# A four-stage network on sixteen images: the front of the next image woven into the scan steps of this one

## The reference

```python
x = x + _L0_conv_ref(_gn(x), qkv_w, proj_w, proj_b)   # attention over 1024 pixels, 6 heads of 32
x = x + _L1_conv_ref(_gn(x), ...)   # selective scan, 4 directions, 192 channels x 16 states
x = x + _L2_conv_ref(_gn(x), ...)   # depthwise 3x3, the top 30 pixels of a channel keep their value
x = x + _L3_conv_ref(_gn(x), ...)   # gated chunked state-space layer, 12 heads
```

## Time and profile before

| | us |
|---|---|
| median of 3 runs | 14195.23 (14193.28 to 14201.19) |
| the profiled execution, its own time | 14205.94 |
| its span | 14204.1 |
| busy in it: PE / DVE / ACT / POOL | 8617.6 / 9455.2 / 4329.4 / 6226.0 |
| mean granted PE clock, share of 2.4 GHz | 0.708 |

### The profile page before, as it was taken

How to read it: one execution, slowest core, us unless ns; L and a number is a source line. 1 busy time by engine, 2 the same in 40 slices (tenths; PEclk the granted TensorE clock), 3 DMA queues, 4 the chain that set the end, 5 groups by cost and what they waited for, 6 DMA issues and landing times. The chain is left out here.

```text
span 14204.1 us, 88128 instructions
## 1 busy us (share of the span) xinstructions
PE 8617.6 (61%) x26672; PEld 2789.1 (20%) x26816; DVE 9455.2 (67%) x8214; ACT 4329.4 (30%) x4371; POOL 6226.0 (44%) x2937
## 2 busy tenths in 40 slices
PE   6475664746647466484664846648466484664846
PEld 2031221212212122121221312213122131221312
DVE  4856748567485674856758577585775857758576
ACT  2323233232332323323233232322323223232232
POOL 1815518155171551715417154271642716427164
PEclk8676776767767677676776767767676676776767
DMA  2505225052250512505135051340513405134061
GB/s 74 138 16 134 55 70 134 16 138 50 75 129 16 142 46 78 126 16 144 44 83 121 16 148 40 85 119 16 151 37 85 119 16 151 37 89 115 16 155 35
DMA packets 364229, 1164.38 MB, mean 82 GB/s; under 512 B 61487, under 2 KB 63039, under 8 KB 363599
## 3 DMA queue, kind: packets, MB, share of 16 engines
q1 hardware_dynamic: 358363, 1155.62, 32.3%
q10 hardware_dynamic: 3988, 1.01, 0.0%
q0 software_dynamic: 1248, 0.64, 0.0%
HBM read 959.86 MB, written 121.63 MB: 76 GB/s over the span
## 5 line engine op out<-in xcount | busy, mean ns | idle before, releaser
L799 PE MATMUL ps<-arena,sel_y 128*32 128x512 f32 x6144 | 2216.9, 888 | 3817.3 <-POOL arena L1048 3817.3
L1048 POOL TENSOR_TENSOR arena<-arena 128x1024 f32<-128x1024 f32 x1536 | 3721.7, 2449 | 29.4 <-DVE arena L995 29.4
L995 DVE TENSOR_TENSOR_SCAN arena<-ps,arena 128x1024 f32<-128x1024 f32 x1536 | 3475.8, 2284 | 66.9 <-POOL arena L1036 22.6
L913 ACT ACTIVATE ps<-arena,v_na 128x1024 f32<-128x1024 f32 x1536 | 1712.4, 1117 | 3797.8 <-DVE arena L995 3110.6
L1036 POOL TENSOR_TENSOR arena<-arena 128x1024 f32<-128x1024 f32 x512 | 1235.4, 2413 | 822.6 <-DMA arena<-scan_dtu 717.5
L799 PEld LDWEIGHTS ps<-arena,sel_y 128*32 128x32 f32 x6144 | 474.5, 151 | 5570.4 <-POOL arena L1048 3509.2
L617 DVE TENSOR_REDUCE arena<-ps 128x1 bf16<-128x1024 f32 x768 | 933.8, 1223 | 922.9 <-PE ps L480 922.4
L1028 POOL TENSOR_TENSOR arena<-arena,XN 128x1024 f32<-128x1024 f32 x32 | 75.2, 2350 | 2839.5 <-DVE arena L942 2839.5
L991 DVE TENSOR_TENSOR arena<-arena,ps 128x1024 f32<-128x1024 f32 x768 | 919.3, 1197 | 565.5 <-DMA arena<-scan_dtu 355.5
L597 ACT ACTIVATE arena<-ps 128x1024 f32<-128x1024 f32 x768 | 744.5, 1021 | 970.6 <-PE ps L532 970.6
L548 PE MATMUL ps<-arena 128*64 128x512 f32 x3072 | 773.0, 627 | 3.5 <-DVE arena L611 3.5
(11 more groups left out here) (213 smaller groups left out, 11961.2 us busy)
## 6 DMA issues: line engine op xcount, KB each, us to landing
arena<-scan_dt SPq DMA_DIRECT2D x768, 512.0 KB, 4.7
arena<-scan_dtu SPq DMA_DIRECT2D x768, 512.0 KB, 6.0
arena<-scan_bc SPq DMA_DIRECT2D x256, 512.0 KB, 6.2
arena<-arena SPq DMA_DIRECT2D x1152, 64.0 KB, 2.0
scan_dt<-arena SPq DMA_DIRECT2D x64, 512.0 KB, 10.9
scan_dtu<-arena SPq DMA_DIRECT2D x64, 512.0 KB, 8.9
scan_dt<-arena SPq DMA_DIRECT2D x64, 256.0 KB, 12.4
scan_dtu<-arena SPq DMA_DIRECT2D x64, 256.0 KB, 12.5
```

The lines of the kernel that those rows point to most:

```text
L799: mm = nc.tensor.matmul(ps[3][32 * q:32 * q + 32, HALF * h:HALF * h + HALF], sel_y[:, r, :], step[i % NBUF][:, HALF * h:HALF * h + HALF], ...
L913: nc.scalar.activation(ps[1 + i % 2][:], dtr[:, i // 2 % RING, :], ACT.Exp, scale=v_na[:, at:at + 1]).then_inc(m_da, 1)
L995: nc.vector.tensor_tensor_scan(step[i % NBUF][:, o], ps[1 + i % 2][:, o], step[i % NBUF][:, o], 0.0, ALU.mult, ALU.add).then_inc(m_h, 1)
L1048: pool.tensor_tensor(step[i % NBUF], step[i % NBUF], Cb[:, 2 * (k // 2) + f, :], ALU.mult).then_inc(m_hc, 1)
```

## The change

The front of an image (group norm, attention, group norm, scan setup) becomes, on each engine, a generator of 192 half steps: `front_sp`, `front_pe`, `front_act`, `front_dve`, `front_pool`. The scan of image b calls `next(front)` twice in each of its 96 steps on every engine, and what comes there is the front of image b + 1. Ahead of the loop the front of image 0 runs alone; the last pass computes a front for a seventeenth image (a copy of the first), which nothing uses.

- **Hand-over.** The image after attention (`after_attention`), the normalised one (`scan_source`), dt, dt * u, B and C go to DRAM in the front and are read back in the next pass; B, C, dt, dt * u had gone there before.
- **Attention.** q and k stay fp32 (QQ, KK), two heads a stack, on rows 0 to 31 and 64 to 95, with a row 32 (96) that holds the maximum and ones; so 12 projections of 512 columns with 24 matmuls instead of six with 12. No bf16 parts, none of the 72 small DMAs, no row copies. The scores of a head are one fp32 matmul of 33 rows (L637) instead of two bf16 ones. Rough scores read the upper half words of the same fp32 (QR, KR). A unit is 512 columns of two heads: PSUM is cut into four banks of 512 for the front, one of them for all rough scores (96 half-row maxima, L820, instead of 48 of 1024), one for sums of heads.
- **Steps.** One PSUM buffer for the decay instead of two (`decay(i + 1)` waits for scan i). b is always read from SBUF. DVE makes 42 inputs (L1073), POOL 54 (L1137). Eight step buffers, dt in a ring of two. PSUM bank `ps[3]` sums states as before.
- **Setup.** In the front: linear part by ACT, clamp and maximum by DVE with both operands in SBUF, all six dt * u by POOL.
- `conv_pool` waits for `f_out`, which SP raises when the front's stores have landed.

The table of half steps: attention's rough scores of the three pairs begin at 16, 52 and 88, units at 52 and 88 (one each two half steps) and 124 (one each half step), projections at 10, output projection at 142, setup from 149 to 184.

```diff
         def scan_pe(pe, front):
...
+            for i in range(NSTEP):
+                next(front)
+                if i % BATCH == 1 and i > BATCH:
+                    sums(i // BATCH - 1)
+                next(front)
+            sums(NSTEP // BATCH - 1)
...
         def scan_act(act, front):
+            def decay(i):
+                _, k, j, _, _, f = STEPS[i]
+                act.wait_ge(m_dtl[i // 2 % DTR], 16 * (i // 2 // DTR + 1))
+                if i:
+                    act.wait_ge(m_h, i)
+                at = 24 * k + 2 * j + f
+                nc.scalar.activation(ps[2][:], dtr[:, i // 2 % DTR, :], ACT.Exp,
+                                     scale=v_na[:, at:at + 1]).then_inc(m_da, 1)
+            decay(0)
+            for i in range(NSTEP):
+                next(front)
+                if i + 1 < NSTEP:
+                    decay(i + 1)
+                next(front)
...
             for i in range(NSTEP):
+                next(front)
                 wait_input(dve, i)
                 dve.wait_ge(m_da, i + 1)
+                nc.vector.tensor_tensor_scan(step[:, i % NBUF, o], ps[2][:, o], step[:, i % NBUF, o], 0.0,
                                              ALU.mult, ALU.add).then_inc(m_h, 1)
+                next(front)
+                if i + 1 < NSTEP and not on_pool(i + 1):
+                    state_input(i + 1)
...
         def on_pool(i):
-            return i % 2 == 1 and i // 2 % 3 != 2
+            return i % 9 not in (1, 3, 5, 7)
```

More of the change, by code:

```diff
@@ L202, in build @@
                       (mask_f[:, :], mask)]
-            two(w_qk, wqk)
+            for h in range(HEADS):
+                t, e = h // 2, h % 2
+                for w, at in ((w_q, 0), (w_k, 128)) if h < 4 else ((w_q, 128), (w_k, 192)):
+                    two(w[:, :, t, 64 * e:64 * e + DH], wqk[:, at + DH * h:at + DH * h + DH])
             two(w_v, wv)
@@ L704, in build @@
-        m_bp = sem("scan_b_block_in_psum")
+        m_du = sem("scan_dtu_ready")
+        m_bw = sem("scan_b_and_c_in_dram")
+        m_wd = [sem(f"scan_dt_in_dram_{u}") for u in range(6)]
+        m_wu = [sem(f"scan_dtu_in_dram_{u}") for u in range(6)]
+        f_x = sem("front_image_in_dram")
+        f_out = sem("front_all_in_dram")
+        HS = 192
+        ROUGH = [16, 52, 88]
+        UNITS = [(52, 2), (88, 2), (124, 1)]
+        DT_AT = (161, 163, 165, 172, 174, 176)
+        LN_AT = (169, 180)
@@ new lines, in build, with bank, unit_at, rough_at @@
+        DT_END = (170, 171, 172, 181, 182, 183)
+        def bank(i):
+            return ps[i // 2][:, HALF * (i % 2):HALF * (i % 2) + HALF]
+        def unit_at(hs):
+            for t, (at, pitch) in enumerate(UNITS):
+                if 0 <= hs - at < 16 * pitch and (hs - at) % pitch == 0:
+                    return t, (hs - at) // pitch
+            return None, 0
+        def rough_at(hs):
+            for t, at in enumerate(ROUGH):
+                if 0 <= hs - at < 36:
+                    return t, hs - at
+            return None, 0
@@ new lines, in _ @@
+            @block.gpsimd
+            def _(pool):
+                for _ in front_pool(pool):
+                    pass
+        clear()
+        with nc.Fori(0, n_batch) as b:
+            with nc.Block() as block:
+                @block.sync
+                def _(sp):
+                    scan_sp(sp, b, front_sp(sp, b + 1))
+                    front_stored(sp)
+                    sp.wait_ge(b_x, 4)
+                    for c, m in enumerate(CT):
+                        sp.dma_start(out[b, 128 * c:128 * c + m, :], X[0:m, c, :]).then_inc(s_out, 16)
+                @block.tensor
+                def _(pe):
+                    scan_pe(pe, front_pe(pe))
+                    norm_pe(pe, 2)
+                    conv_pe(pe)
+                    norm_pe(pe, 3)
+                    mix_pe(pe)
+                @block.scalar
+                def _(act):
+                    scan_act(act, front_act(act))
+                    norm_act(act, 2)
+                    conv_act(act)
+                    norm_act(act, 3)
+                    mix_act(act)
+                @block.vector
+                def _(dve):
+                    scan_dve(dve, front_dve(dve))
+                    dve.wait_ge(m_x, 4)
+                    norm_dve(dve, 2, lambda t, n: XPv[0:n, t, 1:1 + H, 1:1 + W], begun=True, room=k_z)
+                    conv_dve(dve)
+                    dve.wait_ge(k_x, 2)
+                    norm_dve(dve, 3, lambda t, n: XN[0:n, t, :])
+                    mix_dve(dve)
+                @block.gpsimd
+                def _(pool):
+                    scan_pool(pool, front_pool(pool))
+                    conv_pool(pool)
+                    mix_pool(pool)
+            clear()
```

997 lines of the change are left out of this document (490 added, 507 removed).

## The result

| | before | after |
|---|---|---|
| median, us | 14197.35 (14193.28 to 14201.19, 4 runs) | 14317.17 (14303.89 to 14353.96, 4 runs) |
| ratio | | 1.0087, 95% interval 1.0074 to 1.0099 |
| span of the profiled execution | 14204.1 | 14302.1 |
| from one image's first scan to the next one's | 884.5 | 862 |

The change makes the kernel 0.9% slower. The direction was forecast, the size was not: 14590 us and 2.8% were forecast, some three times the measured loss. An image gains 22.5 us, 16 x 22.5 = 360; what lies around the sixteen passes grew from 52 to 510 us, mostly the front that runs alone ahead of the loop, and 458 - 360 is the 98 by which the spans differ.

What follows compares the result with a forecast made beforehand. DVE and POOL were taken to bound the scan steps, PE the attention; merged, they take 628 us. Sixteen times 628 + 255, plus 52, 420 and 2, made 14602, or 14590 us in the runs' measure; range 13450 to 15350.

Steps and rivals of the forecast that it cites:

- The floor of S: Merged stage of front and scan steps: DVE needs about 445 us, POOL 380 us, neither the whole answer.
- the bare step: Scan step without front work: 3.53 us with POOL's input, 4.58 with DVE's, mean 4.0, against 3.7 before.
- I take half the time at each clock: Merged stage: 698 us at 1.2 GHz and 558 at 2.4, half the time at each, giving 628.
- The 1.2 GHz prices of steps 13 to 61: Steps with maxima at the low clock: 80 us for steps 13 to 25, 259 for 26 to 61.
- 4 to 5 us: Steps 26 to 61 at 1.2 GHz: a batch of sums adds this in four steps, less what faster clock returns.
- The share of 2.4 GHz decides, from a mean clock of 0.84: Scan steps: high-clock share sets the time; mean clock 0.84 gives merged stage 603 us, no change.
- Rival A: Clock stays up in the steps, 0.86 of the time at 2.4 GHz: total 13770, faster by 3%; chance 0.36.
- Rival B: Attention: two heads' scores do not overlap and clock stays low; merged stage 707 us, total 15860; chance 0.11.
- 10 until the first rows land: Ahead of the first scan, in the stretch of steps 0 to 4: 10 us until the first rows are loaded.
- 12 because DVE waits for the next image: Steps 0 to 4: DVE waits 12 us for the image behind 7 MB of first loads on SP's queue.
- The first front: Front of image 0, run alone ahead of the loop: 420 us once, from 274 before plus 24, 84 and 38.
- Steps 70 to 95: Last steps: 26 at 4.0 us, 25 of DVE work, 8 of table loads, projections 18 / 5: 155 / 142.

Runs made afterwards that it cites:

- e1: Changed kernel with the woven front left out of the passes, every pass rereading image 0's front results, so images 1 to 15 are not computed: 11399.14 us.
- e4: Changed kernel with fifteen looped passes and the sixteenth written out without the front of a seventeenth image: 14142.52 us, ratio 0.9959 to the kernel before.
- e2: Changed kernel without the rough scores on PE and the 96 half-row maxima on DVE, exponentials unguarded: 13092.69 us.
- e6: Changed kernel with each unit's pair of score matmuls issued twice into the same banks: 15266.23 us.
- e11: Changed kernel with no front in the last pass, later first loads, more POOL inputs, halved sum batches, and no rough scores or maxima: 12785.73 us.
- e12: Changed kernel with the batch of eight sums issued in four parts of two matmuls, one per half step: 14538.00 us, ratio 1.0237 to the kernel before.
- e9: Changed kernel with two extra 128-row fp32 matmuls on PE ahead of each unit's scores: 15133.55 us, ratio 1.0657 to the kernel before.
- e7: Changed kernel with PE issuing the rough score before a unit's scores and sums of heads in a half step: 14626.66 us, ratio 1.0302 to the kernel before.
- e3: Changed kernel with later loads of the second B and C, normalised image and image after attention on SP's queue: 14134.71 us, ratio 0.9955 to the kernel before.
- e8: Changed kernel with the batch of eight sums issued in two halves of four, one per half step: 14096.58 us, ratio 0.9929 to the kernel before.

## Why the prediction was right or wrong

| stretch | forecast, 1.2 / 2.4 GHz (taken) | measured | clock | bare steps (e1) |
|---|---|---|---|---|
| lead-in and steps 0 to 4 | 47 / 47 (47) | 67.9 | 0.50 | 50.9 |
| steps 5 to 12 | 82 / 44 (63) | 44.2 | 0.96 | 32.5 |
| steps 13 to 25 | 80 / 68 (74) | 68.5 | 0.60 | 53.5 |
| steps 26 to 61 | 259 / 205 (232) | 224.8 | 0.69 | 150.2 |
| steps 62 to 69 | 67 / 46 (56.5) | 43.3 | 1.00 | 33.5 |
| steps 70 to 95 | 155 / 142 (148.5) | 151.9 | 0.65 | 104.4 |
| tail and rest | 262 | 261.4 | 0.73 | 255 |
| an image | 883 | 862 | | 680 |
| around the passes | 472 | 510 | | |

Sixteen times -21 is -336, +38 around the passes, and the forecast's 14600 us of span become 14302. The -21 is a sum of errors of both signs: the clock and the prices below made the forecast too long, the lead-in too short. That they left the direction right is in part luck, as the one change of e4 would have turned it.

Some 7 us of the first row belong to the row "tail and rest": the passage between two images, which the forecast had in its 255 us, ends in the lead-in's window here.

- **The floor of S was right, in part by errors that cancel.** DVE busy 445 us was forecast, 446.9 measured; POOL 380, measured 382.3; the bare step 4.0, measured 4.04. Among DVE's terms the inputs were 84.9 and not 94 us, the scalings 20.1 and not 8. The kernel has 43 inputs on DVE and 53 on POOL, not 42 and 54. The old step of 3.7 that this was held against contained the ends of the stage; between first and last scan it was 3.57.
- **The step that failed is "I take half the time at each clock".** It priced every stretch midway between its two ends. But the stretches differed: 0.96 and 1.00 where PE's own work was the long pole, 0.50 to 0.69 elsewhere. Steps 5 to 12 and 62 to 69, whose 1.2 GHz ends lay 38 and 21 us over the others, ran at 0.96 and 1.00 and met the 2.4 GHz ends (44 and 46 forecast, 44.2 and 43.3 measured): these two are -32 us. With the measured clock put in for every stretch, the forecast's own ends give S = 614 instead of 628, so the step as a whole is worth -14. e2, e6 and e11 show that the clock of this stretch was not certain, as the double-paced units can also run at 0.71 to 0.75; in e2 and e11 that cost 10 or 11 us, and not 21.
- **The 1.2 GHz prices of steps 13 to 61 were too high.** With the shares that the clock had (0.60, 0.69), the forecast's own ends give 78 and 238 us; 68.5 and 224.8 were measured. In steps 26 to 61 the "4 to 5 us" for a batch of sums was mis-sized: the nine steps with a batch took 7.9 us in the mean, the others 5.7, so a batch cost 2.2. In steps 13 to 25 the wait behind a batch was 2.9 to 4.3 us, as forecast (3 to 4), but all 13 steps were priced with two maxima, and steps 24 and 25 have none left and took 3.6 us each. The mechanism, DVE waiting behind the batch, is in the trace.
- **"The share of 2.4 GHz decides, from a mean clock of 0.84" fell as a rule.** The steps had a mean clock of 0.70, less than the forecast's 0.75, and were shorter than forecast; e12 and e9 had 0.80 and 0.73 in steps 26 to 61 and were slower, both with more PE work. Rival A did not come. What the runs show in the clock's place is the price of rough scores and maxima, 70 us an image (e2), and of any PE work put between them (e6, e9). That PE and DVE take turns on one PSUM bank is in the waits (e7); a second bank for the rough scores was not tried, so how much of the 70 us is the bank and how much DVE's own 65.5 us of maxima stays open.
- **Rival B is refuted.** A score pair took 1.13 us for four records at 2.4 GHz (four one after the other would be some 1.7), 2.08 at 1.2. The page TensorEngine Tiling (Array Packing) of the Trainium skill, section Key Properties, says that tiles operate independently, and the trace agrees for two row tiles of 33 rows, with the 1.13. The drain on a change of tiling mode, stated there too, can't be told apart from the ordinary tail of 0.2 us in these rows.
- **The lead-in was undersized.** "10 until the first rows land" was 13.5, from SP's first load to the first scan; "12 because DVE waits for the next image" was 20.3. With the 7 us that only moved into this row, and some 2 in the steps, that makes +21. The mechanism (SP's queue with 7 MB of first loads) holds: e3 took 11 us of it back by order alone.
- **The first front was undersized.** 420 us forecast, 449 measured; its score pairs and sums of heads had their 1.2 GHz length up to 412 us, where the forecast had started from a front of before whose loop had 0.96. The rest of the +38 was not traced.
- **Steps 70 to 95 came out for another reason than forecast.** 148.5 against 151.9. The bare steps are right (104 and 104.4). The front adds 47.5 to them: DVE is busy 124.3 us against 86.3, 38 and not 25 us of its work, and the other 10 stand where 13 to 26 were set down for tables and projections. Two errors cancel, which is luck.
- **What was priced at nothing** (the rest, the store of the hand-over, the new waits) cost 1 us: from the first sums taken behind the last scan to the next image's first work, 257.6 us against 256.7 before. The tail, from the last scan's end to there, was 10.4 us and not 8 or 6.

## What to carry to other kernels

Before laying one stage over another, price the bare stage in its new form by itself: here 61 us of slower steps and 10 us of longer gap between images had eaten three quarters of the 93 us by which the woven front was shorter than the old one, and the front run alone cost more than what was left over sixteen images. When two in-order engines hand one PSUM bank back and forth, what stands between two hand-overs on PE is on the path (e6, e8, e9). Shorten pieces, but not so far that their last part comes late for a buffer, nor so that matmuls that ran side by side are cut apart. Don't average over the clock: ask of each stretch whether PE is its bound, and look there first, knowing that the same instructions came at 0.71 in one image and at 1.00 in another (e11).

## What was not expected of the hardware

**DVE and POOL take turns, down to the smallest instruction.** In the timeline of e1 above, DVE's input (two SBUF operands) begins at 2059.94 beside a POOL input that ends near 2061.2, and takes 2.35 us, where the same operation takes 1.20 when it begins before POOL's (at 2282.72 in the changed kernel); POOL's next one begins at 2061.17 and takes 3.33 instead of 2.35. In the changed kernel a group norm's 128x2 product took as long as the POOL operation beside it:

```profile
2712.57 2.34 POOL L1150 TENSOR_TENSOR arena<-arena 128x1024 f32<-128x1024 f32 x1 [3.62 <-DVE arena L1097]
2712.59 2.34 DVE L356 TENSOR_TENSOR g_t<-g_t 128x2 f32<-128x2 f32 x1
```

In the rest of an image, with POOL idle, the same instruction takes 0.16 us. The scalings of attention (L838) were longer too: 1675 ns where the forecast took 684, +12 us an image. The page SBUF — State Buffer of the Trainium skill, section Who interferes with whom, says that a DVE instruction with two SBUF inputs contends with a GpSimd one that reads SBUF. The trace agrees, and here the wait lasted the whole POOL operation, also for 128x2. The maxima, with one PSUM input, kept their 683 ns. A front that is woven beside a busy POOL is therefore dearer on DVE than its rows alone say, and beyond the steps' own inputs (2.05 to 2.23 us there, 1.98 measured) this was not in the forecast.

**The clock is not a function of the instructions alone.** Two images of e11 ran the same eight steps at 0.71 and at 1.00, after 0.82 in both in the stretch before. What set it was not found.

**The granted clock column can mislead at a program's start**: 1.00 up to 420 us in the changed kernel, over score pairs that had their 1.2 GHz length up to 412.
